# A matrix of 32x32 products in a delta-rule kernel: its sixteen groups become the innermost dimension

## What is computed

```
x = x + 0.5 * ffn(layernorm(x))
x = x + attn(layernorm(x))
x = x + 0.5 * ffn(layernorm(x))
...
diff = Gg[:, :, :, None, :] - Gg[:, :, None, :, :]
Dts = exp(where(mask, diff, -inf))
Mi = [einsum('bhtsd,bhsmd->bhtsm', kg[..., i, :] * Dts, w) for i in range(Rr)]
M = tril(stack(Mi).reshape(b, h, C * Rr, C * Rr), k=-1)
u = solve_triangular(M, rhs, lower=True, unit_diagonal=True)
attn = einsum('bhtsd,bhsmd->bhtsm', qg[:, :, :, None, :] * Dts, w)
o = SCALE * (o_inter + einsum('bhtsm,bhsmv->bhtv', attn, u))
```

## Time and profile before

| what | value |
|---|---|
| median of 3 runs | 4855.98 us |
| the profiled execution's own time | 4860.39 us |
| its span, first to last instruction | 4858.6 us |
| steps of the delta phase | 64 |
| instructions | 168256 |
| mean granted TensorE clock | 0.982 |

### The profile page before, as it was taken

One profiled execution on the slowest core, in us unless ns is written; L12 is line 12 of the kernel. 1 busy time (PEld: TensorE's weight loads), 2 busy tenths in 40 slices (PEclk: granted clock), 3 DMA queues, 4 the chain that ended last, 5 costly groups with the idle time before them and its releaser, 6 DMA issues. The chain is left out here.

```text
span 4858.6 us, 168256 instructions
## 1 busy us (share of the span) xinstructions
PE 4468.0 (92%) x71392; PEld 3187.2 (66%) x71392; DVE 3944.4 (81%) x7007; ACT 3601.1 (74%) x6897; POOL 3191.9 (66%) x5572
## 2 busy tenths in 40 slices
PE   8869999999999999999999999999999999999898
PEld 5536666666666666666666666666666667666665
DVE  3278898888988888888888888888888988888522
ACT  3367887788877888878888778877788777888431
POOL 0037777777777777777777777777777777777600
PEclk9979999999999999999999999999999999999799
DMA  2200000000100000000100000000000000000100
GB/s 89 88 29 25 26 26 15 25 26 26 35 22 25 30 26 26 17 23 26 35 33 30 14 26 26 26 26 15 30 31 26 26 15 25 26 26 9 38 9 22
DMA packets 49790, 136.49 MB, mean 28 GB/s; under 512 B 7056, under 2 KB 28176, under 8 KB 48400
## 3 DMA queue, kind: packets, MB, share of 16 engines
q1 hardware_dynamic: 49040, 125.73, 7.4%
HBM read 111.56 MB, written 14.16 MB: 26 GB/s over the span
## 5 line engine op out<-in xcount | busy, mean ns | idle before, releaser
L1563 DVE SCALAR_TENSOR_TENSOR acc<-bank,vc,acc 128x510 f32<-128x510 f32 (+2 forms) x1728 | 1270.8, 739 | 97.2 <-ACT acc L1188 68.2
L2006 POOL TENSOR_TENSOR LZ<-LZ,LT 128x120 f32<-128x120 f32 (+26 forms) x1984 | 981.6, 495 | 155.4
L2003 POOL TENSOR_TENSOR LT<-LA,LZ 128x120 f32<-128x120 f32 (+26 forms) x1984 | 931.6, 470 | 145.9
L1560 DVE TENSOR_TENSOR X<-KQ,Fl 128x640 f32<-128x640 f32 x1024 | 930.2, 918 | 15.6 <-ACT Fl L1189 15.6
L1953 POOL TENSOR_TENSOR kdec<-KQ,Fe 128x256 f32<-128x256 f32 x512 | 447.4, 895 | 622.7 <-PE bank L909 622.7
L1188 ACT ACTIVATE Us<-bank 128x128 f32<-128x128 f32 x1024 | 271.0, 275 | 582.2 <-PE bank L838 582.0
L1977 POOL TENSOR_TENSOR X<-KQ,F 128x512 f32<-128x512 f32 x256 | 361.8, 1413 | 482.2 <-ACT F L1189 280.0
L838 PE MATMUL bank<-xnTm,WK 128*128 128x512 f32 x1280 | 632.1, 617 | 45.9 <-DVE acc L1563 39.1
L838 PEld LDWEIGHTS bank<-X 128*32 128x32 f32 x24576 | 402.8, 112 | 165.9 <-issue 88.8
L838 PE MATMUL bank<-xnTm,WV 128*128 128x512 f32 x1024 | 502.2, 613 | 1.5 <-DVE acc L1563 1.3
L838 PE MATMUL bank<-X 128*32 128x20 f32 x24576 | 495.0, 200 | 4.8 <-DVE X L1560 3.9
(11 more groups left out here) (148 smaller groups left out, 9727.0 us busy)
## 6 DMA issues: line engine op xcount, KB each, us to landing
WK<-in_wkq SPq DMA_DIRECT2D x64, 704.0 KB, 5.4
WV<-in_wv SPq DMA_DIRECT2D x64, 576.0 KB, 3.8
WO<-in_wo SPq DMA_DIRECT2D x64, 128.0 KB, 2.0
wuh<-in_wu SPq DMA_DIRECT2D x2, 1024.0 KB, 7.4
xt<-in_x SPq DMA_DIRECT2D x4, 512.0 KB, 6.6
wuh_d<-wuh SPq DMA_DIRECT2D x1, 2048.0 KB, 6.3
x_d<-x SPq DMA_DIRECT2D x4, 512.0 KB, 3.1
xnT_d<-xT SPq DMA_DIRECT2D x4, 512.0 KB, 2.7
```

Of the source, the lines that this page charges most:

```text
L1560: return e.tensor_tensor(o, a, b, op)
L1563: return e.scalar_tensor_tensor(out=o, in0=a, scalar=sc, in1=b, op0=op0, op1=op1)
L2003: e.tensor_tensor(tmp, LA[:, j + 1:32, 8 * (j % R) + j // R].unsqueeze(2).broadcast_to([P, rr, cc]), LZ[:, j, 0:cc].unsqueeze(1).broadcast ...
L2006: e.tensor_tensor(LZ[:, j + 1:32, 0:cc], LZ[:, j + 1:32, 0:cc], tmp, SUB).then_inc(g_row, 1)
```

## The change

The matrix is stored as `[P, 5, 8, 16]`: kind, token, group column. The stride in the group column is one word, that in the token is 16 words (64 bytes) and that in the kind is 128 words. The views of `Pd` are rewritten so that every instruction reads and writes the same elements in the same order as before, with other strides. No instruction is added, removed or moved on any engine, and every wait stays. The masks and `LA` keep their layouts.

```
-        Pd = sb("Pd", [P, 16, 5, 8])
+        Pd = sb("Pd", [P, 5, 8, 16])
...
-                pd = Pd[:, n]
-                rows = pd.rearrange("p n i t -> p (n i) t")
-
-                def put(o, m, cols, d, c):
-                    mk = cs[:, m:m + cols].bitcast(U32).rearrange("p (n c) -> p n c", c=c)
+                pd = Pd[:, :, :, n]
+                quads = pd.rearrange("p i (a c b) n -> p n (i a) c b", a=2, c=2)
+
+                def put(o, m, d, c):
+                    mk = cs[:, m:m + 80].bitcast(U32).rearrange("p (n a c) -> p n a c", n=4, c=c)
                     return e.copy_predicated(o, mk, d.rearrange("p n (a c) -> p n a c", c=c))
...
-                    e.copy_predicated(pd.rearrange("p n i (a c) -> p n c i a", c=2), mk,
+                    e.copy_predicated(pd.rearrange("p i (a c) n -> p n c i a", c=2), mk,
                                       src[:, :, 0:40].rearrange("p n (c i a) -> p n c i a", c=2, a=4)).then_inc(v_Pd, 1)
...
-                    put(pd.rearrange("p n i (a c b) -> p (n i a) c b", a=2, c=2)[:, :, 1, :], C_M1, 80,
-                        src[:, :, 40:60], 2).then_inc(v_Pd, 1)
+                    put(quads[:, :, :, 1, :], C_M1, src[:, :, 40:60], 2).then_inc(v_Pd, 1)
...
-                    put(rows[:, :, 4:8], C_M2, 80, src[:, :, 60:80], 4).then_inc(v_Pd, 1)
+                    put(pd.rearrange("p i t n -> p n i t")[:, :, :, 4:8], C_M2, src[:, :, 60:80], 4).then_inc(v_Pd, 1)
...
-                                  Pd[:, :, 4, :].unsqueeze(2).broadcast_to([P, 16, 4, 8])).then_inc(v_bd, 1)
+                                  Pd[:, 4].rearrange("p t n -> p n t").unsqueeze(2).broadcast_to([P, 16, 4, 8])).then_inc(v_bd, 1)
...
-                            Pd[:, :, 0:R, :].rearrange("p n i t -> p (i t) n").unsqueeze(2)
+                            Pd[:, 0:R].rearrange("p i t n -> p (i t) n").unsqueeze(2)
                             .broadcast_to([P, 32, 2, 16])).then_inc(v_in, 1)
```

## The result

The changed kernel takes 4874.32 us, the median of 4 runs (4871.42 to 4882.03), against 4857.01 for the kernel before on the same chip. It is not inside the range of the case that the number stands for (4889 to 4936).

The account below looks back on a forecast made before the run. TensorE, busy 92% of the span, was taken as the bound. Terms 0.10 + 0.25 + 0.52 = 0.87 us a step, times 64 steps = 55.7 us, gave 4916.1, or 4911.7 us at the runs' median; range 4858 to 4936.

Parts of the forecast that it names:

- the case that the number stands for: Evacuations priced by 16-byte lines begun: slower, 4911.7 us, own range 4889 to 4936, chance 0.50.
- by the line: Evacuations' writes cost 4.4 ns per added 16-byte line: +0.35, +0.18 and +0.26 us for first, second and third; chance 0.50.
- Take counted at 0: Take, 0.93 us shorter per step, gains nothing: its gain ends in idle time before the reciprocal, which waits for kn.
- b = 1, +0.52: Longer evacuations at b = 1 delay TensorE 0.52 us a step: 0.09 from the first, 0.17 second, 0.26 third.
- b = 0, +0.25: Evacuations at b = 0 grow 0.70 us, 0.50 left after cover; half counted, +0.25 us a step, ends 0 and 0.50.
- b = 2, 0: Evacuations at b = 2 grow 0.80 us, counted at 0 because TensorE has other work there.
- b = 3 with take, 0: Evacuations ahead of take grow 0.35, 0.18, 0.26, take saves 0.93: -0.14 us, ending in idle time, counted at 0.
- Diagonal, +0.10: Diagonal's strided read of Pd costs 0.47 us more, most absorbed by slack; +0.10 us a step, ends 0 and 0.35.
- GpSimd's rows start behind the reciprocal, so they move with nothing.: GpSimd's rows, starting behind the reciprocal, were taken not to move with the change; no cost counted.
- The number 4912: Predicted time of the changed kernel, 4911.7 us, from 0.87 us a step over 64 steps.
- by the word: Rival: a word of an unfilled line costs 1.94 ns, so only third evacuations grow; 13 us slower, 4869; chance 0.25.

Follow-up runs that it names:

- The probe: Kernel before with single 80-word predicated copies and products at several strides ahead of the phase; predicated write 246, 332, 507 ns for 20, 40, 80 blocks; no total time given.
- b = 0 alone: Kernel before with only the three evacuations of b = 0 writing with the change's strides, take and diagonal as before: ratio 1.0044 [1.0032, 1.0056].
- the diagonal alone: Kernel before with only the diagonal reading Pd with the change's strides, all writes and take as before: ratio 1.0004 [0.9995, 1.0012].
- the kernel with the swap: Kernel before with VectorE's product X of levels(p - 1, 3, 4) moved behind clamp(p), no stride changed: 4831.67 us, ratio 0.9944 [0.9931, 0.9956].

## Why the forecast was right and wrong

- *Durations of take and evacuations, "by the line".* Right: 1246 for 1239 ns, 873 for 860, 502 for 500. The probe gives 4.3 and 4.4 ns a block for the 4.4 taken from three rows. (0.18 / 40 is 4.5 ns and not 4.6; nothing hangs on it.)
- *Take counted at 0.* Right, alone: 1.0000. With the evacuations, which use up the idle time ahead of the reciprocal, it may give up to 7 us, which the intervals do not separate from nothing.
- *b = 1, +0.52.* Right at its place, 0.47 (0.14 to 0.61 in the table) and 0.48 alone, though TensorE's wait there rose to 0.60 us and not to near 0.8. Wrong as a term of the sum, because of what follows behind it: alone it costs 0.0028, 13.6 us or 0.21 a step.
- *b = 0, +0.25.* Right at the products of b = 1, where TensorE is 0.28 us late with b = 0 alone. Over the step 1.0044, 21 us or 0.33, a mean over steps of 67.1 us and steps of up to 67.8 and more that differ by who has the turn at kdec.
- *b = 2, 0.* Measured 7 us faster. The cover was there, and what moved behind it was not looked at.
- *b = 3 with take, 0.* Not contradicted; the evacuations of b = 3 without the faster take cost 1.0012, 6 us.
- *Diagonal, +0.10, of a read priced at 0.47 us.* The read cost 0.31 us, and the term has the wrong sign: about -16 us in the changed kernel, 0 alone.
- *"GpSimd's rows start behind the reciprocal, so they move with nothing."* This is **the step that failed**: a term put at nothing. GpSimd does not wait for Pd, but each of its instructions that read SBUF takes turns with VectorE's two-input ones. With the diagonal alone its row LZ went from 813 to 1135 ns, and with one swap of VectorE's order the second half of kdec went from 1.31 to 0.72 us. All of my costs were waits on semaphores, added up one by one. The rule of turns in the Trainium skill (SBUF — State Buffer, Who interferes with whom) bore on it, and I had weighed only the one on strides. The spread was in the profile, and I did not ask for it: the earlier trace rows show X at 0.82 us, and the groups of the kernel before a mean of 918 ns:

```profile
L1560 DVE TENSOR_TENSOR X<-KQ,Fl 128x640 f32<-128x640 f32 x1024 | 930.2, 918 | 15.6 <-ACT Fl L1189 15.6
```

- *The sum again, in us a step.* Forecast 0.87. The diagonal takes 0.28 off (from +0.10 to -0.18, the 0.79 and 0.61 at b = 1), and the evacuations of b = 0 and b = 1 add 0.02 (0.79 for 0.77). Between b = 1 and Ys 0.08 go, which I did not look into, and at kdec 0.20, of which 0.10 go without the diagonal too. That leaves 0.33, or 21 us, for a measured 17 (interval 13 to 25).
- *The number 4912.* The change costs some 54 us over the kernel with the swap, for the 56 forecast. That is luck: 24 of the 54 are a longer wait for kdec, which the sum does not have. And 4874 lies nearer to the 4869 of "by the word" than to my number, also by luck: that case is refuted by the second evacuation, which takes 0.51 us and not 0.33.

## What to carry to other kernels

Before adding up waits, compare the shortest and the mean duration of each two-input VectorE instruction and of each GpSimd instruction of one shape. Where they differ, look in the timeline for turns between the two engines: an edit that shifts one of them by a few hundredths of a microsecond can exchange who pays, and that can be worth more than what the edit saves or costs. Look first at the GpSimd instruction that the bound engine waits for, and keep VectorE's two-input instructions away from it: one swapped line was worth 27 us here, more than the whole change of layout cost. But it was worth nothing in the changed kernel, where another instruction stood in the same place, so look again after every edit. Before a layout is turned for one reader, price the masked writes by the 16-byte blocks that they touch.

## What the hardware showed that I had not expected

- A masked copy of 80 words costs by the 16-byte block it writes, 246, 332 and 507 ns for 20, 40 and 80, from PSUM and from SBUF (251, 336, 511); a plain product costs at most 303.
- In a turn one keeps its time and the other pays; they do not share. Of X and the row beside it, the one that starts first keeps its time (0.83, 0.43 us), and the other pays (1.06, 1.10). Within some 0.02 us the recorded starts no longer tell who is first: with b = 0 alone both orders occur in one kernel, and the steps differ by 0.7 us.
- So a delay of GpSimd of 0.30 us vanished in the next row, and one of 0.09 us came through to TensorE in full. With one of 0.18 us, in the changed kernel, TensorE's wait of 0.19 us for S was gone.
